# A hybrid attention and feed-forward kernel: the semaphore waits of the window scores move one product ahead, and a semaphore increment of TensorE goes

## The reference

```python
x = x + _L0_attn_a_ref(_layernorm(x), ...)   # chunked linear attention, 8 heads
x = x + _L0_ffn_ref(_layernorm(x), ...)      # 6 layers of local attention and gated feed-forward
x = x + _L0_attn_b_ref(_layernorm(x), ...)   # retention
x = x + _L0_ffn_ref(_layernorm(x), ...)      # the 6 layers again
```

```python
def attn_layer(x, Wqkv, qs, ksc, Wo):            # 16 heads of 64
    q, k, v = jnp.split(x @ Wqkv, 3, -1)
    q, k = l2norm(q) * qs, l2norm(k) * ksc
    ... rotary position with a scale on q and k ...
    out = local_attention(q, k, v)               # windows of 32 queries, 64 keys, softmax
    return out @ Wo
def ffn_layer(x, g, bln, W1, b1, W2, b2):
    xn = layernorm(x) * g + bln
    a, gate = jnp.split(xn @ W1 + b1, 2, -1)     # 341 channels each
    return a * jax.nn.gelu(gate, approximate=False) @ W2 + b2
for i in range(6):
    x = attn_layer(shift_tokens(x), ...) + x
    x = ffn_layer(shift_tokens(x), ...) + x
```

## Time and profile before

| | |
|---|---|
| median of 3 runs | 3218.97 us (3210.69 to 3222.32) |
| the profiled execution, its own time | 3213.76 us |
| its span, first to last instruction | 3211.9 us |
| TensorE busy, matmul | 2949.8 us (92%) |
| VectorE busy | 2877.9 us (90%) |
| ScalarE busy | 2445.2 us (76%) |
| GpSimd busy | 1808.5 us (56%) |
| mean granted TensorE clock | 0.985 of full speed |

### The profile page before, as it was taken

One profiled execution on the slowest core, in us unless ns is written; L12 is line 12 of the kernel. 1 busy time (PEld: TensorE's weight loads), 2 busy tenths in 40 slices (PEclk: granted clock), 3 DMA queues, 4 the chain that ended last, 5 costly groups with the idle time before them and its releaser, 6 DMA issues.

```text
span 3211.9 us, 93327 instructions
## 1 busy us (share of the span) xinstructions
PE 2949.8 (92%) x37516; PEld 1832.0 (57%) x37516; DVE 2877.9 (90%) x2670; ACT 2445.2 (76%) x3899; POOL 1808.5 (56%) x823
## 2 busy tenths in 40 slices
PE   8699999999999999999998999999999999999996
PEld 4356555555655555655555556555556555655653
DVE  5599999999999999999999889999999999999994
ACT  4578788787887878877676678887788887887774
POOL 8555556555555565655444455555556555555651
PEclk9799999999999999999999999999999999999998
DMA  9544544544544544553343354445445444444442
GB/s 319 174 112 105 147 110 115 142 114 103 149 120 101 144 119 100 148 136 97 94 125 89 89 137 117 117 117 133 113 120 132 113 124 130 111 119 130 125 110 57
DMA packets 254405, 398.04 MB, mean 124 GB/s; under 512 B 51148, under 2 KB 84872, under 8 KB 254280
## 3 DMA queue, kind: packets, MB, share of 16 engines
q1 hardware_dynamic: 254280, 396.41, 47.1%
HBM read 64.64 MB, written 19.92 MB: 26 GB/s over the span
## 4 chain that ended last, share of the span: by engine, by line
DVE 42%; ACT 26%; issue 15%; PE 11%; SPq 1%; POOL 1%; DVEq 1%; DMA 1%; ACTq 0%; POOLq 0%
DVE f_w L1351 8%; DVE f_p L1386 6%; DVE f_rs L1380 5%; DVE f_rn L1361 5%; ACT f_p L1112 4%; DVE f_w L1356 4%; PE ps L810 3%; DVE f_mx L1371 3%; DVE f_p L1374 3%; PE ps L828 3%; ACT ps L1099 3%; ACT f_u L1087 3%; ACT f_ab L1088 3%; DVE f_ab L1365 2%; ACT f_hid L1145 2%
## 5 line engine op out<-in xcount | busy, mean ns | idle before, releaser
L1305 POOL TENSOR_TENSOR f_ab<-f_w,f_rn 128x1024 f32<-128x1024 f32 x192 | 593.6, 3092 | 452.7 <-DVE f_rn L1361 435.9
L1300 POOL TENSOR_TENSOR f_w<-f_w,f_ab 128x1024 f32<-128x1024 f32 x192 | 549.3, 2861 | 526.2 <-DVE f_w L1351 526.2
L1296 POOL TENSOR_TENSOR f_u<-f_u 128x512 f32<-128x512 f32 x384 | 589.9, 1551 | 350.5 <-ACT f_u L1087 348.6
L1088 ACT ACTIVATE f_ab<-ps,f_pa 128x512 f32<-128x512 f32 x768 | 543.1, 707 | 1.2
L1087 ACT ACTIVATE f_u<-ps 128x512 f32<-128x512 f32 x768 | 467.7, 609 | 76.0 <-PE ps L790 70.4
L1351 DVE TENSOR_TENSOR f_w<-f_ab,f_tan 128x1024 f32<-128x1024 f32 x384 | 501.4, 1346 | 3.5 <-POOL f_ab L1305 2.3
L788 PE MATMUL ps<-f_xh,f_wh 128*128 128x512 f32 x768 | 403.6, 526 | 65.5 <-ACT f_ab L1088 56.1
L849 PE MATMUL ps<-f_tb,f_v 128*64 128x160 f32 (+1 forms) x6144 | 442.8, 297 | 17.8 <-DMA f_tb<-f_pt 13.3
L849 PEld LDWEIGHTS ps<-f_tb,f_v 128*64 128x64 f32 x6144 | 396.6, 138 | 109.2 <-issue 74.2
L1099 ACT ACTIVATE ps<-ps 128x512 f32<-128x512 f32 x384 | 204.9, 575 | 303.3 <-PE ps L810 303.3
L828 PEld LDWEIGHTS ps<-f_kb,f_qb 64*32 64x32 f32 x24576 | 278.1, 106 | 220.0 <-issue 213.4
(11 more groups left out here) (163 smaller groups left out, 4839.1 us busy)
## 6 DMA issues: line engine op xcount, KB each, us to landing
f_kb<-f_ab SPq DMA_DIRECT2D x384, 256.0 KB, 3.6
f_qb<-f_ab SPq DMA_DIRECT2D x384, 256.0 KB, 3.6
f_tb<-f_pt SPq DMA_DIRECT2D x1344, 64.0 KB
f_wh<-split_w SPq DMA_DIRECT2D x48, 384.0 KB, 4.4
f_wl<-split_w SPq DMA_DIRECT2D x48, 384.0 KB, 4.2
a_w_raw<-wqkv SPq DMA_DIRECT2D x24, 384.0 KB, 4.6
split_w<-a_w_hi SPq DMA_DIRECT2D x24, 384.0 KB, 4.5
split_w<-a_w_lo SPq DMA_DIRECT2D x24, 384.0 KB, 5.4
```

What stands on the lines that cost most here:

```text
L1088: nc.scalar.activation(ab[:, g % 2, i, :], bank("qk", g, i), ACT.Identity, scale=pa[:, g, i:i + 1]).then_inc(qk_read.sem, 1)
L1296: nc.gpsimd.tensor_tensor(u[:, 2 * i + 1, :], u[:, 2 * i, :], u[:, 2 * i + 1, :], ALU.add).then_inc(sq_sum[i].sem, 1)
L1300: nc.gpsimd.tensor_tensor(w[:, 0:2, :], w[:, 0:2, :], ab[:, k % 2, 0:2, :], ALU.add).then_inc(q_sum.sem, 1)
L1305: nc.gpsimd.tensor_tensor(ab[:, k % 2, 0:2, :], w[:, 0:2, :], rn[:, 0:1, :].broadcast_to([128, 2, N]), ALU.mult).then_inc(rope_q.sem, 1)
```

## The change

The three waits leave `scores` and become a function of their own, `scores_ready`. In the retention steps it is called directly ahead of `scores`, which leaves the waits where they were. In the ordinary steps it is called one product earlier, so that the last whole-array product in front of the scores stands behind the waits: for that `project_out` and `hidden` can now be called in parts. The increment of `scores_begun` and that semaphore are removed.

```diff
-        scores_begun = sem("scores_begun")
...
-                        def scores(g):
+                        def scores_ready(g):
+
+                            pe.wait_ge(m_ready.sem, now.count(m_ready, g))
                             pe.wait_ge(q_dma.sem, now.count(q_dma, g))
                             pe.wait_ge(k_dma.sem, now.count(k_dma, g))
 
-                            pe.wait_ge(m_ready.sem, now.count(m_ready, g))
-                            pe.sem_inc(scores_begun, 1)
+                        def scores(g):
+
                             for tile in range(TILES):
...
-                        def project_out(g):
+                        def project_out(g, parts=range(2)):
...
-                            for i in range(2):
+                            for i in parts:
...
-                        def hidden(kind, first, ready):
-                            for j in range(3):
+                        def hidden(kind, first, ready, parts=range(3)):
+                            for j in parts:
...
                         if prev:
-                            project_out(1)
+                            project_out(1, (0,))
+                            scores_ready(-1)
+                            project_out(1, (1,))
                             scores(-1)
...
-                            project(2, range(4))
+                            project(2, range(3))
+                            scores_ready(0)
+                            project(2, (3,))
                             scores(0)
...
                             project(3, (0, 1))
+                            scores_ready(1)
                         if prev:
                             mean()
                         if cur:
...
-                            hidden("val", 0, val_ready)
+                            hidden("val", 0, val_ready, (0, 1))
+                        if cur:
+                            scores_ready(2)
+                        if prev:
+                            hidden("val", 0, val_ready, (2,))
                         if cur:
                             scores(2)
```

## The result

The changed kernel takes 3276.4 us (median of 4 runs, 3273.8 to 3280.2), the kernel before 3214.8 (4 runs, 3210.4 to 3222.3). The ratio is 1.019, with a 95% interval of 1.0165 to 1.0215: 61.6 us slower. The profiled execution of the changed kernel took 3280.2 us, 3.8 more than the median, so what is counted in its trace is a little more than what a median execution has.

A forecast was written before the change was run, and what follows sets the result against it. It took a dependence ring through ScalarE, TensorE and VectorE at the step's end as the bound. 3213.8 + 40 (product behind the wait) + 28 (clock falls) = 3282; 3284 us predicted with the median's footing, range 3248 to 3303.

The forecast's parts named there:

- The sum: Whole kernel: 3213.8 + 40 + 28 = 3282 us for an execution like the profiled one; 3284 predicted.
- What bounds the kernel: End of an ordinary step: a dependence ring from ScalarE's mask through TensorE's scores and norms and ScalarE's roots to VectorE's L1361.
- The increment: Behind the waits ahead of the scores: removing it gives nothing; its whole price cannot be over 0.24 us.
- Quads -1, 0 and 1: Their waits, one product earlier in ordinary steps, cost nothing; quad 1's mean may start 0.4 us later, off the chain.
- First term: Quad 2, 42 ordinary steps: third val product behind the mask wait delays the scores 0.96 us each, 40 us (26 to 45).
- VectorE stays ahead: At L1361: VectorE, with 0.76 us to spare, waits about 1 us for the third val product but still arrives first.
- Second term: TensorE's hole before quad 2's mask grows to 2.22 us; clock falls in 25 steps, 1.1 us each, 28 us (0 to 71).
- The delay alone: Rival: the product's delay costs 26 to 45 us and the clock stays up, 3240 to 3264 us; chance 0.27.
- The rival that the change makes no difference: Rival: slack at VectorE's L1361 hides the wait, or the compiler puts it behind the third product; 3205 to 3232 us, chance 0.07.
- The faster one: Rival: issue between mask and end of scores leaves the chain, 0.25 us a call, 42 us gained, 3172 us; chance 0.04.
- What would show it: Signs in ordinary steps: mask wait moves to L884, L1361 still idles, step about 63 us or 64 with a fall, clock about 0.97.

The follow-up runs named there:

- the first experiment: Changed kernel with quad 2 of the ordinary steps as before, all three val products ahead of the waits and its increment kept: 3211.9 us against 3213.1, ratio 0.9994.
- the filled hole: Changed kernel with two whole-array products, whose output nobody reads, added ahead of quad 2's wait in ordinary steps: 3249.7 us, ratio 1.011.

## Why the prediction was right, point by point

*The sum.* It gave 68 us over the kernel before (3282 against 3213.8); 61.6 were measured, 66.5 between the spans of the two profiled executions. The absolute time, 3276.4, is 8 below the forecast 3284 also because the kernel before measured 3214.8 and not the 3219 of the first three runs.

*What bounds the kernel.* Shown. A piece put between mask and scores came out in the time nearly whole (65 us by the stretches, 66.5 by the spans), and a mask moved forward gave 35.5 us.

*The increment: nothing. Quads -1, 0 and 1: nothing.* For the three quads both are shown together by the first experiment, 0.9994. They were not tried one by one: their sum lies between 0.15% faster and 0.03% slower, and two effects of opposite sign aren't excluded. For quad 2 the term is right in this change and not by the reason given. From the mask to the product behind it 0.23 us pass without the increment and 0.24 with it; but where the scores stand directly behind the wait it costs 0.2 us of the 0.24 that the prediction named as its highest price, as the retention steps show.

*First term, 40 us.* The mechanism held, and what was off is its size: 0.81 us a step by the stretches (34 us), 36.7 us by the filled hole. Of its parts the product was put at 1.06 us, from load to load, and costs 0.99 from first pass to first pass (1050.72 to 1051.71, where the first passes of the scores begin with their loads). The faster scores were put at 0.1 us and give 0.18: the loads of the scores begin at 1051.71 and those of the norms at 1053.19, 1.48 us, where they took 1.66. So part of the 0.25 us comes back and not all, more than the rows of quad 1 had made me take. The Trainium skill ("TensorE: Matmul & The Clock Gate", the table at its head) states a queue of 64 that pulls weight loads ahead; the prediction had worked out from it that all of the 0.25 us would come back and the term be 34 us. The trace agrees with the 34 by number only: 0.99 less 0.18 happens to be the same as 1.06 less 0.25.

```profile
1051.71 1.38 PEld L829 LDWEIGHTS ps<-f_kb,f_qb 64*32 64x32 f32 x128 [0.79 <-issue]
1053.19 0.30 PEld L809 LDWEIGHTS ps<-f_u,f_ones 128*128 128x128 f32 x2
```

*VectorE stays ahead.* Right. Its reserve at L1361 was 0.76 us and is 0.59 at L1375 in the steps without a fall, since the third L1409 comes later by a little more than L1375 does.

*Second term, 25 falls of 1.1 us, 28 us.* The falls are 26 in the profiled execution, at 1.21 us each (8.08 less 6.87), 31 us; between the changed kernel and the one with the hole filled lie 25 to 27 us by the medians. The hole was forecast at 2.22 us and is 2.20. That the count came out so close is luck: it was put between two holes, and nothing in the rows gave a share of three in five. The sentence that 2.22 us is less than any hole after which the clock fell is wrong, too. Outside the ordinary steps the trace of before has shorter ones: behind a hole of 1.83 us at 87.52 the clock was at half speed from 87.8, and behind one of 2.09 at 3188.24, with another of 1.44 following, from 3190.5.

```profile
87.52 1.86 PE L225 MATMUL ps<-a_osq,a_blockmask 128*128 128x512 f32 x2 [1.83 <-ACT a_osq L305]
3188.24 1.13 PE L873 MATMUL ps<-f_fs,mean_w 128*128 128x512 f32 x2 [2.09 <-ACT f_fs L1122]
```

*The rivals.* The delay alone (3240 to 3264) is what the kernel with the filled hole measures, 3249.7. It failed because the clock does fall at a hole of 2.20 us. The rival that the change makes no difference would have needed slack at L1361, which isn't in the rows. The faster one counted on issue time on the chain, and 0.2 us a call of that are real where the scores stand directly behind a late wait; but in the ordinary steps the product stands there and costs 0.81.

*What would show it.* All of it came. The step grew to some 62.7 us without a fall (62.69 in the kernel with the hole filled, median of its steps), a little less than the 63 forecast, in line with the first term, and to 63.9 with one.

## What to carry to other kernels

On a chain that sets the pace, move a wait ahead of a product only where it is over, or nearly, when it is reached: ask of each wait who releases it and when, and leave in front of a late one all the work that fits in its hole. Between a late wait and its product even an increment is on the chain (0.2 us here). A hole on TensorE can cost twice, by its length and by the clock of what stands behind it, and work that nobody reads can be worth its place there (some 25 us here). The waits that tell this are few and regular: one idle gap per step, ended by one ScalarE instruction, was the place where 62 us were lost and 35 us could be won by reordering ScalarE.

## What was not expected of the hardware

The loss by one fall of the clock hardly depends on when it comes: in the 26 steps the fall began from 0.1 to 1.7 us behind the end of the mask, and the stretch to L1375 was 7.9 to 8.2 us in all of them, though the slow time covered the `val` product and the scores in some and the norms in others. And a hole of nearly the same length in every step (2.20 us, 2.02 in the last three) was followed by a fall in 26 steps of 42 and not in the rest; one of 3.06 us (2.88 in the last three), in 34 of 42. Of the three steps with 2.02 us, two had a fall. So it isn't the length of the hole alone that decides, and what else does was not tested here.
